# Order of work at the start, at the passage into the FFN and at the last store of a cross-attention and mixture-of-experts kernel

## The reference

```
x  = x + Attn(q from LN(x), k and v from ctx)      # 16 heads of 16, biases, softmax(q k / 4)
xt = LN(x);  logits = xt @ Wg.T;  top1 = argmax over 8 experts
xhat = LN(xt)
y  = sum over experts e of [top1 == e] * (gelu((xhat*s_e + b_e) @ W1_e + b1_e) @ W2_e + b2_e)
out = x + y
```

## Time and profile before

| | us |
|---|---|
| median of 3 runs | 1419.14 (1418.70 to 1420.74) |
| the profiled execution, in all | 1419.81 |
| its span, first to last instruction | 1418.0 |
| TensorE busy (PE) | 1385.2, 98% of the span |
| VectorE (DVE) | 1160.4, 82% |
| ScalarE (ACT) | 986.7, 70% |
| GpSimd (POOL) | 486.0, 34% |
| mean granted TensorE clock | 0.994 |

### The profile page before, as it was taken

How to read it: one execution, slowest core, us unless ns; L and a number is a source line. 1 busy time by engine, 2 the same in 40 slices (tenths; PEclk the granted TensorE clock), 3 DMA queues, 4 the chain that set the end, 5 groups by cost and what they waited for, 6 DMA issues and landing times.

```text
span 1418.0 us, 40277 instructions
## 1 busy us (share of the span) xinstructions
PE 1385.2 (98%) x15394; PEld 1200.7 (85%) x15394; DVE 1160.4 (82%) x2757; ACT 986.7 (70%) x1668; POOL 486.0 (34%) x667
## 2 busy tenths in 40 slices
PE   7899999999999999999999999989999999999998
PEld 6788888888888888888888888877888888888887
DVE  4788888888888888888888888876887887888775
ACT  4577777777777777777777777756766666676663
POOL 4223332233223332233223332324544544444430
PEclk9999999999999999999999999999999999999999
DMA  5657765667557765666566765643343444434322
GB/s 161 171 150 184 180 172 150 185 167 180 143 156 180 179 160 151 178 170 179 152 161 177 181 159 147 161 118 104 98 129 106 120 112 114 124 103 133 106 76 75
DMA packets 173671, 207.47 MB, mean 146 GB/s; under 512 B 20087, under 2 KB 125866, under 8 KB 173482
## 3 DMA queue, kind: packets, MB, share of 16 engines
q1 hardware_dynamic: 173482, 204.89, 54.5%
HBM read 69.26 MB, written 33.81 MB: 73 GB/s over the span
## 4 chain that ended last, share of the span: by engine, by line
PE 89%; DVE 5%; ACT 2%; issue 2%; DMA 1%; SPq 0%; POOL 0%; ACTq 0%; DVEq 0%; POOLq 0%
PE s_ps L1382 13%; PE pp_ps L1253 11%; PE pv_ps L1201 8%; PE st_ps L1184 8%; PE s_ps L1156 8%; PE pp_ps L1226 7%; PE st_ps L1407 7%; PE pp_ps L1261 6%; PE pp_ps L1407 6%; PE pv_ps L1209 4%; PE pp_ps L1247 3%; DVE negmax L860 2%; PE pp_ps L1346 2%; PE t_ps L1175 2%; PE t_ps L1357 1%
## 5 line engine op out<-in xcount | busy, mean ns | idle before, releaser
L667 ACT ACTIVATE pT<-st_ps 128x1024 f32<-128x1024 f32 x256 | 262.9, 1027 | 102.7 <-PE st_ps L1184 101.5
L860 DVE TENSOR_REDUCE negmax<-s_ps 128x8 f32<-128x1024 f32 x256 | 311.3, 1216 | 21.3 <-PE s_ps L1156 21.2
L517 POOL TENSOR_TENSOR q_parts<-q,q_parts 128x1024 bf16<-128x1024 f32 x31 | 66.4, 2140 | 395.3 <-ACT q_parts L661 395.3
L725 ACT ACTIVATE pT<-s_ps,c 128x512 f32<-128x512 f32 x128 | 87.8, 689 | 115.9 <-PE s_ps L1382 112.7
L1156 PE MATMUL s_ps<-k_packed,q_packed 96*128 96x128 bf16 x2048 | 158.3, 220 | 7.0 <-DVE negmax L860 4.9
L1382 PE MATMUL s_ps<-k_packed,w_hi 128*128 128x512 f32 x512 | 165.0, 413 | 0.0
L1184 PE MATMUL st_ps<-q_packed,k_packed 98*128 98x128 bf16 x2048 | 158.6, 221 | 0.0
L1156 PEld LDWEIGHTS s_ps<-k_packed,q_packed 96*128 96x128 bf16 x2048 | 128.3, 98 | 25.6 <-DVE negmax L860 16.5
L1184 PEld LDWEIGHTS st_ps<-q_packed,k_packed 98*128 98x128 bf16 x2048 | 121.0, 98 | 25.5 <-issue 25.5
L535 POOL TENSOR_TENSOR xb<-xin,bo_all 128x256 f32<-128x256 f32 x128 | 90.4, 727 | 146.4 <-DMA x_scratch<-xb 131.4
L1201 PE MATMUL pv_ps<-pT,v 128*32 128x128 f32 x4096 | 138.5, 276 | 0.0
(11 more groups left out here) (203 smaller groups left out, 3699.1 us busy)
## 6 DMA issues: line engine op xcount, KB each, us to landing
q_packed<-q_parts SPq DMA_DIRECT2D x186, 256.0 KB, 4.2
k_packed<-k_parts SPq DMA_DIRECT2D x186, 256.0 KB, 4.5
xin<-in_x_dram SPq DMA_DIRECT2D x32, 512.0 KB, 4.0
cin<-in_ctx_dram SPq DMA_DIRECT2D x32, 512.0 KB, 4.5
out_dram<-xb SPq DMA_DIRECT2D x32, 512.0 KB, 3.2
x_scratch<-xb SPq DMA_DIRECT2D x32, 256.0 KB, 4.8
x_scratch<-xb SPq DMA_DIRECT2D x64, 128.0 KB, 4.6
k_parts<-mask_scratch SPq DMA_DIRECT2D x32, 256.0 KB, 4.1
```

The source lines that it names most:

```text
L667: a.activation(pT[u % 2][:], st_ps[:], ACT.Exp, scale=DH ** -0.5).then_inc(s_exp, 1)
L725: a.activation(hidden32[m], h_ps[m % 2], ACT.Gelu, bias=c1[:, m:m + 1]).then_inc(f_he, 1)
L860: v.tensor_reduce(own, s_ps[:].rearrange("p (h s) -> p h s", s=P), AX_X, ALU.max, negate=True).then_inc(s_red, 1)
```

## The change

Five places are re-ordered or cut differently. No arithmetic changes, and the only instructions added are two DMA issues.

1. TensorE, start: items 0 and 1 of group 0 come before the two bias transposes, items 2 and 3 behind them.
2. ScalarE, start: `normalise(1)` comes before the copy of item 8 of group 0.
3. VectorE, step 0 of group 0: the maxima of unit 3 come first, then the remainder, then the eight FFN bias additions, which were ahead of the group before.
4. VectorE, passage: the statistics of FFN group 0 go from step 6 to step 5 of group 30, those of FFN group 1 from step 3 to step 5 of group 31, and `split_xT(0)` from step 6 to step 7 of group 31, ahead of `keep_logits(0)`.
5. SP: the last group's output is stored as batches 0 and 1, batch 2, and batch 3, each as soon as its additions are done; the final wait counts two more DMAs.

```diff
-            def store(n):
-                dst = out_v[n]
-                sp.wait_ge(f_out, at(GB, n, GB))
-                sp.dma_start(dst, xb[n % 2][:]).then_inc(f_st[n % 2], 16)
+            def store(n, first=0, stop=GB):
+                sp.wait_ge(f_out, at(GB, n, stop))
+                sp.dma_start(out_v[n][:, first:stop, :], xb[n % 2][:, first:stop, :]).then_inc(f_st[n % 2], 16)
...
-                store(n)
+                    store(n)
+                else:
+                    store(n, 0, 2)
+                    store(n, 2, 3)
+                    store(n, 3, GB)
...
-                sp.wait_ge(f_st[n], 8 * GROUPS)
+                sp.wait_ge(f_st[n], 8 * GROUPS + (32 if n == LAST % 2 else 0))
...
             mid(0, 1)
+            normalise(1)
             item(0, 8)
-            normalise(1)
             item(0, 9)
...
             remainder(1, 4)
-            dve.wait_ge(s_c1T, 1)
-            for m in range(MC):
...
-            last.then_inc(s_c1, 1)
+            def ffn_bias():
+                dve.wait_ge(s_c1T, 1)
+                for m in range(MC):
...
+                last.then_inc(s_c1, 1)
...
+                    if n == 0 and u == 0:
+                        maxima(0, 3)
                     if more and u < 3:
                         remainder(n + 1, 5 + u)
+                    if n == 0 and u == 0:
+                        ffn_bias()
...
-                    if later(n, u, 3):
+                    if later(n, u, 3) and (n, u) != (0, 0):
                         maxima(*later(n, u, 3))
...
-                    if n == LAST - 1 and u == 6:
+                    if n == LAST - 1 and u == 5:
                         ffn_stats_of(dve, 0)
-                    if not more and u == 3:
+                    if not more and u == 5:
                         ffn_stats_of(dve, 1)
-                    if not more and u == 6:
+                    if not more and u == 7:
                         split_xT(0)
-                    if not more and u == 7:
                         keep_logits(0)
...
                 turn_weight(k)
+            item(0, 0)
+            item(0, 1)
             pe.wait_ge(s_rows, 16 * 4)
             t.transpose(pv_ps[:, 0:NR], rows[:], ident[0:NR, 0:NR])
             pe.wait_ge(s_rowh, 1)
             t.transpose(pv_ps[:, NR:NR + 2 * C], rows_h[:], ident[0:2 * C, 0:2 * C]).then_inc(s_rowT, 1)
-            for k in range(4):
-                item(0, k)
+            item(0, 2)
+            item(0, 3)
```

More of the change, by code:

```diff
@@ L1038, in _ @@
             remainder(1, 4)
-            dve.wait_ge(s_c1T, 1)
-            for m in range(MC):
[L1041 to L1044, removed]
-            last.then_inc(s_c1, 1)
+            def ffn_bias():
+                dve.wait_ge(s_c1T, 1)
+                for m in range(MC):
+                    for e in range(EC):
+                        r = slice(e * HID, (e + 1) * HID)
+                        last = v.tensor_tensor(c1[r, m:m + 1], pv_ps[r, EC * m + e:EC * m + e + 1],
+                                               cols[r, 3 * C + m:3 * C + m + 1], ALU.add)
+                last.then_inc(s_c1, 1)
             def group(n):
```

## The result

| | before | after |
|---|---|---|
| median | 1420.08 (1418.70 to 1422.77, 8 runs) | 1412.36 (1410.03 to 1416.51, 8 runs) |
| ratio | | 0.9948, 95% interval 0.9937 to 0.9960 |
| profiled execution | 1419.81, span 1418.0 | 1414.05, span 1412.1 |
| TensorE busy, granted clock | 1385.2, 0.994 | 1384.3, 0.995 |

Faster by 7.4 us (5.7 to 8.9) by the ratio; the forecast was 1412.7. TensorE's share of the chain that ended last is the same 89%. To see where the time went, four points are followed that exist in both kernels: the first transposes of group 2, where TensorE begins to be always busy; the scores with a wait of 0.7 us in step 5 of group 30; the one-hot transposes of the first FFN group; the last pair of additions.

What follows compares the result with a forecast made beforehand. The prediction took TensorE to bound the kernel, with 89% of the chain that ended last. Its terms, 0.3 + 0 + 2.7 + 1.0 + 1.1 + 1.3 = 6.4 us, off 1419.14 gave 1412.7; 8-in-10 range 1410.4 to 1416.2.

Steps and rivals of the forecast that it cites:

- (a): Start, TensorE: two x transposes ahead of the bias transposes start 0.57 us earlier at half speed, worth 0.3 us.
- (b): Start, ScalarE: normalising group 1 before the value copies removes a 1.24 us wait, but a DMA is late next; worth 0.
- (c): Step 0 of group 0, VectorE: fourth unit's maxima first cut the 3.82 us wait; 2.7 us left at 62.75.
- (d1): Passage, group 30: FFN group 0 statistics a step earlier; 0 directly, 1.0 us from a clock that stays up.
- (d2): Passage, group 31: later group 1 statistics and split_xT remove waits of 1.05 and 0.85 us; 1.1 us left.
- (e): Tail: last output in three stores leaves only 128 KB behind the last addition, worth 1.3 us.
- less than 2.5 us from last issue to landing: Tail: sign expected in the changed profile for the last store, once the output goes in three stores.
- The estimate of 0.9: Tail: gain from 384 KB fewer at 436 GB/s by the skill's formula; the sum would be 0.4 us smaller.
- The middle: From about 63 us to the passage: TensorE never idle for long, so it gives nothing and keeps earlier savings.
- R4: Attention groups: rival that all 28 lock at a slower 29.21 us each, costing 8.7 us, to 1421.4; chance 0.05.
- R1: Start: rival that the gain of (c) is absorbed by something not moved, giving 1415.4; chance 0.11.
- R2: Passage: rival that the FFN moves only shift stalls, (d1) and (d2) giving 0, so 1414.8; chance 0.11.

Runs made afterwards that it cites:

- fill: 100 small bf16 matmuls, results unused, in TensorE's early waits: ratio 0.9985 on the kernel before, 0.9943 on the changed kernel, 0.9927 on that without (b).
- (c) alone: Kernel before with only the fourth unit's maxima put ahead of the remainder and the eight bias additions: 1416.31 us, ratio 0.9984.
- the two series of times: The changed kernel against the kernel before, measured and later repeated unedited: ratios 0.9948 and 0.9953.
- (c), (d1), (d2) and (e) alone: Four kernels, each the kernel before with only that one part of the change: ratios 0.9984, 0.9995, 0.9997 and 1.0000.

## Why the prediction was right, and where its sizes were off

- **(a)** predicted 0.3. In the compared pair VectorE's low part starts 0.17 earlier, and 0.14 is left at the remainder that opens the filling (43.73 and 43.59). At the first scores it is worth about 1 us over the executions with and without it, as said above. The term that was mis-sized is "spent at half speed until the clock rises at the same moment": the clock at the start is not the same in every execution (0.54 to 1.00 with (a)), and behind the first scores it fell only where (a) was in, which the forecast did not have.
- **(b)** predicted 0, with a loss if the longer gap costs the clock. The wait became 2.02 us and the clock fell behind it (0.88, then 0.63, from 31.6 to 38.5), and by 43.6 us about 0.45 of the 0.60 that the first scores had gained were gone. But the fall came without (b) too, so this loss is not shown to be (b)'s. In the times, with and without fill, (b) is not shown to be worth anything; filled, the ratio without it is the better one (0.9927 and 0.9943), with overlapping intervals.
- **(c)** predicted 2.7 where the chains meet, 3.0 with (a). Measured 3.08. The steps held: split 0.17, transpose at 45.97 (46.3), scores at 50.77 (51.1), a fall of the clock behind the new gap (from about 51.2, where "after 52" was said). (c) alone had no such fall and needed 1.5 us less from the first scores to group 2.
- **(d1)** predicted 0 directly and 1.0 by the clock. Measured 0.17 and 1.55 in this pair: between the two score blocks 13.98 us before, 12.43 in the executions with the old place and no fall, 12.26 with (d1). The 1.3 that I called the most was passed; it was read from a stretch that ends at 945.80, and the low clock went on behind it (0.50 up to 946.0, 0.71 from 946 to 947). The before of this pair was one of the executions in which the clock fell, so that the 1.0 came true is in part luck.
- **(d2)** predicted 1.1. Measured 1.62: 0.4 us of waiting for the last exponential came as 0.32, and the low part of xT held nothing up, where 0.2 to 0.5 was charged. The reason stands in these lines, the first three from the kernel before and the last three from the changed one:

```profile
960.15 0.20 POOL L581 TENSOR_TENSOR rstd<-rstd 128x4 f32<-128x4 f32 x1
964.31 0.68 DVE L1004 TENSOR_TENSOR k_packed<-q,k_packed 128x512 fp32r<-128x512 f32 x1
964.47 1.65 POOL L589 TENSOR_TENSOR k_packed<-q,k_packed 128x512 fp32r<-128x512 f32 x1 [3.62 <-DVE k_packed L1001]
...
960.31 0.69 DVE L1007 TENSOR_TENSOR k_packed<-q,k_packed 128x512 fp32r<-128x512 f32 x1
960.51 0.54 POOL L584 TENSOR_TENSOR rstd<-rstd 128x4 f32<-128x4 f32 x1
961.50 1.29 POOL L592 TENSOR_TENSOR k_packed<-q,k_packed 128x512 fp32r<-128x512 f32 x1
```

The 1.65 us that were carried over are the length beside VectorE's low part; begun clear of it, the same instruction takes 1.29, in all seven executions with (d2). By the Trainium skill ("Advanced Engine Details and Errata", GPSIMD Details) GpSimd shares an interface with VectorE and conflicts with its instructions that have two SBUF inputs; the forecast warned that this could cost what (d2) brings. The trace agrees in the passage too, but GpSimd started second and was the one held up (0.54 us instead of 0.20), off the path.
- **(e)** predicted 1.3. From the start of the last addition to the end of the span, seven executions with (e) took 3.57 to 3.88, seven without it 4.39 to 4.77: 0.9 by the means (3.70 and 4.58). The mis-sized step is the landing: a store of 128 KB took 1.7 us in a quiet stretch, and the last one 2.9 here (2.6 to 3.0 in the seven), behind the two before it; the sign "less than 2.5 us from last issue to landing" failed. The estimate of 0.9 from the Trainium skill ("DMA: Bandwidth & Descriptors", Anatomy of one DMA) was nearer than my row. That is in part luck: the section gives its formula for DMAs issued by GpSimd, and these are SyncE's; and it would put the two stores of the earlier trace rows 0.9 us apart, where they are 1.8 apart (3.5 and 1.7).
- **The middle** was put at nothing and cost 1.20 in the compared pair. It has the same code in all fourteen profiled executions and took 870.70 to 873.40 in them (before: 872.05), so this lies within what single executions differ by. The slower rhythm of R4 would have added 8.7; none had it.

The terms, 6.4 in all, stand against 3.08 + 0.17 + 1.55 + 1.62 + 0.68 - 1.20 = 5.9 in the traces, and 7.4 (5.7 to 8.9) and 6.7 (4.5 to 8.8) in the two series of times. That the trace comes so near the sum is partly luck: (d1) and (d2) brought 1.2 more than was said, the tail and the middle 1.8 less. One slip of the forecast changes nothing: R1 and R2 together come to 1417.5 by its terms, not 1417.8. What stays open: (c), (d1), (d2) and (e) alone add up to 3.4 us by their ratios (each uncertain by about 1.5, the sum by about 3), and the whole is twice that. (a) is the candidate for the rest, and it was only run once. Only (c) is shown in the times by itself; the shares of the others are read from traces.

## What to carry to other kernels

Where an engine falls idle in a thin stretch, ask which of its waits is made by a collision in time rather than by a dependence: here moving 1.33 us of cheap work and a remainder behind an urgent 8-column operation took away a wait of 3.8 us. Compare profiles only with several executions of each kernel at hand, since the same start differed by 1.1 us and the same middle by 2.7. And where thin stretches cost the clock, filling them can be tried: in the kernel before it gave 2.1 us (0.7 to 3.5), less than the edits.

## What the runs showed of the hardware

- A two-input VectorE operation of 128x8 that started together with a GpSimd operation of 128x1024 lasted as long as this in one execution (2.14 and 2.12 us); in five others the first half, which started with it, went through in 0.17, and the second, 0.2 us later, took 1.97; begun 0.11 us ahead of GpSimd's, such an operation took 0.17 (one execution). Where GpSimd started second it was held up: its 128x4 operation took 0.54 us instead of 0.20 when it started 0.20 us behind a VectorE operation of 128x512 that lasted 0.69 (seven executions), and its 128x512 operation 1.65 instead of 1.29 when it started 0.16 us behind one (seven against seven).
- Whether the clock falls is not settled by the stretch alone: in 939.4 to 942.8 TensorE was busy 1.41 us in the kernel before and 1.40 in the same kernel filled at the start; in the first the next stretch was granted 0.55, in the second 1.00. Over 59 executions of the kernel before, the time goes with the mean granted clock: 1421.9 us on average at 0.992 (6 runs), 1420.0 at 0.993 (19), 1419.5 at 0.994 (17), 1417.6 at 0.995 (9), 1416.6 at 0.996 (6).
